# Gather-and-experts stage: order of its loads, and returned rows and experts one round later

## The reference

```
# L3_xattn_ref(ctx_4096, _layernorm(x), affine_w, affine_b)
idx = jax.lax.top_k(-pdist, K)[1]                      # 16 nearest of the context's features
gathered = jnp.take_along_axis(feat, flat_idx[:, None, :], axis=2)
lap = gathered.reshape(Bn, K, Nn * Fd)
out = jnp.einsum('bkm,k->bm', lap, affine_w) + affine_b[0]
...
# L3_ffn_ref(_layernorm(x), gate_w, lora_A, lora_B)
gate_probs = jax.nn.softmax(x @ gate_w.T, axis=-1)
weights, sel = jax.lax.top_k(gate_probs, TOP_K)
...
for e in range(N_EXPERTS):
    y = x @ lora_A[e].T @ lora_B[e].T
    out = out + w_full[:, e:e + 1] * y
...
x = x + jnp.tanh(g_xattn[3]) * _L3_xattn_ref(ctx_4096, _layernorm(x, axis=-1), ...)
x = x + jnp.tanh(g_ffn[3]) * _L3_ffn_ref(_layernorm(x, axis=-1), ...)
```

## Time and profile before

| | |
|---|---|
| median of 3 runs | 3380.32 us (3369.56 to 3383.47) |
| profiled execution | 3379.05 us |
| its span | 3377.4 us |
| busy: PE, DVE, ACT, POOL | 2917.9, 2090.3, 1129.3, 462.0 us |
| mean granted clock of PE | 0.93 of full |
| this stage | 2997 to 3377 us of the span |

### The profile page before, as it was taken

The page is one execution under the profiler, slowest core; times in us unless marked ns, Lnnn a source line. Parts: engine busy times, 40 slices in busy tenths (PEclk is TensorE's granted clock), DMA queues, the critical chain, the costliest instruction groups (busy, mean ns, idle before and its releaser), DMA issues. The chain is left out here.

```text
span 3377.4 us, 55656 instructions
## 1 busy us (share of the span) xinstructions
PE 2917.9 (86%) x20468; PEld 2057.5 (61%) x20468; DVE 2090.3 (62%) x3684; ACT 1129.3 (33%) x2348; POOL 462.0 (14%) x540
## 2 busy tenths in 40 slices
PE   7999999999964999785999999999778888847888
PEld 4666566566642788663565555665567677635664
DVE  5544544554447667554665655665578888946774
ACT  3333343333331233222544344544333223211222
POOL 0111011011022000000221122211222322200000
PEclk9999999999987999977999999999888988867999
DMA  6100110010034455353333222331410000035441
GB/s 229 43 31 12 42 43 31 11 42 31 5 104 158 133 141 142 94 185 130 113 123 124 74 87 94 117 106 56 154 38 23 18 18 18 22 100 183 155 142 45
DMA packets 102177, 288.77 MB, mean 86 GB/s; under 512 B 33352, under 2 KB 56552, under 8 KB 92432
## 3 DMA queue, kind: packets, MB, share of 16 engines
q1 hardware_dynamic: 70928, 166.09, 14.9%
q0 software_dynamic: 22160, 103.47, 9.5%
q10 hardware_dynamic: 8848, 16.10, 1.8%
HBM read 242.57 MB, written 43.04 MB: 85 GB/s over the span
## 5 line engine op out<-in xcount | busy, mean ns | idle before, releaser
L2043 PE MATMUL bank<-ffn_qT,ffn_wgu 128*128 128x112 bf16 x4096 | 244.4, 230 | 57.3 <-DVE ffn_gs L2226 48.8
L2043 PEld LDWEIGHTS bank<-ffn_qT,ffn_wgu 128*128 128x128 fp8e4 x4096 | 240.3, 108 | 63.6 <-issue 61.1
L1462 DVE TENSOR_REDUCE latent_nmax<-bank 112x1 f32<-112x487 f32 x128 | 85.2, 666 | 270.2 <-PE bank L1327 262.7
L2173 POOL TENSOR_TENSOR ffn_h<-ffn_sl,ffn_us 128x448 f32<-128x448 f32 x64 | 136.7, 2135 | 406.2 <-ACTq L2128 227.7
L1288 PEld LDWEIGHTS bank<-latent_hT,latent_wq 128*128 128x128 f32 x1536 | 180.4, 195 | 9.5 <-issue 9.1
L1661 PE MATMUL bank<-grouped_kT,grouped_qT 128*112 128x375 f32 x512 | 178.8, 492 | 6.2 <-ACT grouped_probs L1782 5.9
L1288 PE MATMUL bank<-latent_hT,latent_wq 128*128 128x112 f32 x1536 | 179.6, 278 | 0.0
L1251 POOL TENSOR_SCALAR latent_probs<-latent_probs,latent_rsum 112x487 f32<-112x487 f32 x128 | 88.1, 688 | 658.6 <-DVE latent_rsum L1467 658.6
L2127 ACT ACTIVATE ffn_sl<-ffn_gs,ffn_sgu 128x112 f32<-128x112 f32 x256 | 78.4, 376 | 292.6 <-DVEq L2228 292.5
L1815 POOL TENSOR_SCALAR grouped_probs<-grouped_probs,grouped_rsum 112x375 f32<-112x375 f32 x256 | 147.2, 594 | 173.4 <-DVE grouped_rsum L1893 173.4
L1266 PE MATMUL bank<-latent_wv,latent_hT 128*125 128x384 f32 (+1 forms) x512 | 168.3, 490 | 0.0
(11 more groups left out here) (398 smaller groups left out, 5902.4 us busy)
## 6 DMA issues: line engine op xcount, KB each, us to landing
grouped_raw<-L_weights POOLq DMA_DIRECT2D x24, 2048.0 KB, 8.5
points_spread<-numbers SPq DMA_DIRECT2D x32, 912.0 KB
codes<-grouped_code SPq DMA_DIRECT2D x24, 512.0 KB, 4.3
latent_hT<-ctxT SPq DMA_DIRECT2D x8, 1500.0 KB, 6.8
plain_ctxT<-ctxT POOLq DMA_DIRECT2D x8, 1500.0 KB, 16.5
plain_ctx<-ctx POOLq DMA_DIRECT2D x8, 1500.0 KB, 34.7
grouped_ctxT<-ctxT SPq DMA_DIRECT2D x8, 1500.0 KB, 12.2
latent_xy<-planes SPq DMA_DIRECT2D x8, 1024.0 KB, 8.4
```

The source lines that it names most:

```text
L2043: mm = pe.matmul(ahead.tile(t)[:, i * Q:(i + 1) * Q], wgu[:, u0 + f // 4, c:c + P], qT[:, k, :], start=(k == 0), stop=(k == KC - 1))
L2173: pool.tensor_tensor(h[:, G * j:G * j + G, :], sl[:, j % 2], us[:, j % 2], ALU.mult).then_inc(h_ready, 1)
```

## The change

ACT instead of SP issues x of batch 0, ahead of the constants. SP sends set 0 of batch 0 at once and the others after x and the constants have landed. POOL sends aT and gT after 14 one-hots instead of 6, and bT after 26, with a semaphore of its own. `returned` goes from k = 9 to k = 10, `update` from k = 11 to k = 12, and all steps of the experts one round later.

```diff
-    ROUNDS = U + 12 + 22
+    ROUNDS = U + 13 + 22
...
-        weights_loaded = s_.sem("weights_loaded")
+        weights_loaded, output_loaded = s_.sem("weights_loaded"), s_.sem("output_loaded")
...
-            return [(m, t) for m in range(B) for t in (u - 16 * (m + 1) - 12,) if 0 <= t < 22]
+            return [(m, t) for m in range(B) for t in (u - 16 * (m + 1) - 13,) if 0 <= t < 22]
...
-            if k == 9 and 1 <= b <= B:
+            if k == 10 and 1 <= b <= B:
                 order += [(("back", b - 1, i), 6 + i) for i in range(2)]
...
-            sp.dma_start(x[:, 0, :], x_in[0]).then_inc(x_loaded[0], 16)
             for b in range(B):
                 for c in range(4):
+                    if (b, c) == (0, 1):
+                        sp.wait_ge(x_loaded[0], 16)
+                        sp.wait_ge(consts_loaded, 80)
                     if b >= 1:
                         sp.wait_ge(onehot_ready, (b - 1) * K + 4 * (c + 1))
...
-            pool.wait_ge(onehot_ready, 6)
+            pool.wait_ge(onehot_ready, 14)
             pool.dma_start(aT[:], fold(A["L3_lora_AT"])).then_inc(weights_loaded, 16)
             pool.dma_start(gT[:], fold(A["L3_ffn_gate_wT"])).then_inc(weights_loaded, 16)
-            pool.dma_start(bT[:], fold(A["L3_lora_BT"])).then_inc(weights_loaded, 16)
+            pool.wait_ge(onehot_ready, 26)
+            pool.dma_start(bT[:], fold(A["L3_lora_BT"])).then_inc(output_loaded, 16)
...
-                        pe.wait_ge(weights_loaded, 48)
+                        pe.wait_ge(weights_loaded, 32)
...
                 if t == 15:
+                    if m == 0:
+                        pe.wait_ge(output_loaded, 16)
                     pe.wait_ge(hT_ready, m + 1)
...
-                if k == 9 and 1 <= b <= B:
+                if k == 10 and 1 <= b <= B:
                     returned(b - 1)
...
+            act.dma_start(x[:, 0, :], x_in[0]).then_inc(x_loaded[0], 16)
             act.dma_start(wcol[:], A["L3_xattn_affine_w"]).then_inc(consts_loaded, 16)
...
-                if k == 11 and 1 <= b <= B:
+                if k == 12 and 1 <= b <= B:
                     update(b - 1)
```

## The result

The changed kernel takes 3403.88 us (median of 6 runs, 3399.6 to 3405.99), the kernel before 3381.89 beside it (3369.56 to 3384.72): a ratio of 1.0071, 95% interval 1.0051 to 1.0091. On a second occasion it was 1.0043 (1.002 to 1.0065). It is slower; 3368.5 was forecast.

What follows compares the result with a forecast made beforehand. Late constants bound the start, the spread stream the starved stretch, PE and DVE in turns the later rounds. Terms 2.5 + 9.6 - 0.5 = 11.6 us less gave 3368.5 us; range 3356 to 3380, the forecast's own 3363 to 3374.

Steps and rivals of the forecast that it cites:

- x and constants first: Stage's start: x and the constants land near 3008, so first DVE work comes 6.6 us earlier, ends 0 and 9.6.
- SP's new wait: Start, batch 0's sets: DMA engines idle 2.8 us, one-hot 12 stalls 0 to 1 us; costed at nothing.
- Weights later: Starved stretch up to one-hot 32: of the start's 6.6 us gain 2.5 remain, one-hot 32 at 3088.9 against 3091.45.
- Returned rows: Later rounds: one round more gives the load 1.2 to 2.5 us; five waits, 7.6 us, lie in batches 2 to 6.
- Experts one round later: Later rounds: a batch takes 36.0 instead of 38.1 us; 9.6 us less over batches 2 to 7, ends 0 and 14.
- Tail: After 3326: batch 6's shift behind the last maximum and one addition costs 0.5 us, ends -2 and 0.
- the fourth: Rival, slower: bT in flight starves batch 1's last set and batch 2's sets, PE's clock stays low; 3392 us, chance 0.04.

Runs made afterwards that it cites:

- e13: e10 with x of batch 0 and the constants first on ScalarE's queue, without SP's wait; first DVE work at 20.8 us of the stage, ratio 0.996.
- e1: The changed kernel with the rounds put back as before, so only the loads changed; ratio to the kernel before 0.999, stage 374.8 us.
- e3: The changed kernel with ScalarE's copy of the turned rows put ahead of the square root; ratio to the kernel before 0.9966, later rounds 224.3 us.
- e7: The kernel before with one line moved, ScalarE's square root from round k = 3 to k = 2; ratio 1.0078, later rounds 257.4 us.
- e6: e3 with `update` back at k = 11; ratio to the kernel before 0.9956, later rounds 213.2 us.
- e10: The kernel before, its loads unchanged, with the rounds of e6; 3366.71 us (median of 12 runs), ratio to the kernel before 0.996.

## Why the prediction was wrong, point by point

1. *x and constants first.* Right: first DVE work at 11.7 us of the stage, 10.7 forecast (3008 against 2997.3); 5.6 us won where 6.6 was taken. SP's wait brought it and not the move of x to another queue (e13).
2. *SP's new wait, costed at nothing.* Somewhat low: one-hot 12 waited 1.43 us in the changed kernel and up to 4.33 in the six profiles with its loads, where a stall of 0 to 1 was forecast. The idle time of the DMA engines behind the wait was sized rightly: their share is 0.01 and 0.00 from 3020 to 3022 and near 0.4 again from 3023, which fits the 2.8 us taken.
3. *Weights later, 2.5 us left at one-hot 32.* 2.4 in the first profile, but 0.0 in the second (94.2 against 94.2, the mean of before) and -2.0 on the mean of six. That the spread stream decides and eats the start's gain was right. In the first profile one-hots 16 to 32 came within 2 us of the times forecast; in the others they came later, and why is open. So the term of 2.5 us is not confirmed: e1, the loads alone, has a ratio of 0.999 (0.997 to 1.0009). bT had landed before PE asked for it.
4. *Returned rows.* The waits went, as forecast: none in the changed kernel's later rounds.
5. *Experts one round later, -9.6 us.* This step failed. The order of one batch was laid out for PE and DVE, and ScalarE's queue was left out, although the step moved one of its instructions, the copy of the turned rows, into a round in which its program first waits for DVE; and it had no term for the wait for the table's bank. Measured: 245.4 and 245.1 us for the later rounds against 230.7 and 223.6, so 14.4 to 21.8 us more where 9.6 less stood. The mechanism has two places: the copy behind the root (e3: 21 us back; e7: the same loss from one line), and the table's bank behind `update` (e6: 11 us back). By PE's busy time in the windows shown, about half of the first (9.6 of 20.3 us) and all of the second is clock, which the step did not have in it. The rest of the layout was right: with both places mended, a batch in e10 takes 35.7 to 35.9 us where 36.0 was laid out, and the later rounds take 212 to 214 us, 9 to 19 below the two executions of before.
6. *Tail, -0.5.* Within what two executions differ by: 54.1 and 55.2 against 55.2.

Of the rivals the fourth named the right side, but its mechanism (bT starving batch 2) is not the one: e1 shows the loads alone at 0.999. The range missed because no rival had a new wait in a queue that nobody had laid out, and because nothing was added for PE's clock: the one batch that the step was worked out from had run at 1.00 throughout, while others of the same execution had not.

## What to carry to other kernels

When steps of a software pipeline move by a round, write down for every engine, the lightly loaded ones too, what then stands ahead of each step in that round and what it waits for; here an engine busy for 55 of 245 us held up the others. A bank or buffer freed in the round in which it is wanted again is a wait. And a wait of PE costs more than itself where its clock falls behind it: price it with the matmuls that follow at half clock.

## What the runs showed of the hardware that was not expected

PE's granted clock fell to its lower level behind single idle times of 2.30 us and 0.61 us (both in the changed kernel's rows above), in the first case some 1.5 us after work had started again, and was back at 1.00 in the window from 3290. The Trainium skill, TensorE: Matmul & The Clock Gate, Part 1, names the same two levels. The length of the last wait alone does not decide. In the kernel before, the 1.10 and 1.44 us in the earlier trace rows passed without a fall, but the clock fell behind these two waits for the returned rows, at 3157 and at 3198:

```profile
3156.32 1.09 PE L2442 MATMUL bank<-const_ident,points_back 128*112 128x128 f32 x8 [2.15 <-DMA points_back<-flat]
...
3198.13 1.84 PE L2442 MATMUL bank<-const_ident,points_back 128*112 128x128 f32 x8 [1.33 <-DMA points_back<-flat]
```

In e10 a wait of 1.33 us stands in every batch, and the clock is 1.00 in every window of 1 us from 3119 to the last one-hot:

```profile
3154.73 0.60 PE L516 MATMUL bank<-const_ident,points_zm 112*128 112x112 f32 x4 [1.33 <-DVE points_x L2664]
```

What the engine had done over a longer time before each wait was not varied, so what decides is open.

Untouched stages of 3000 us moved by 20 us between executions (2995.8 to 3016.2), more than the 16.3 us by which the change lengthened its stage; a single pair of profiles would have charged 12.6 us of that to the change.
